# A macaron block with 32 experts: the down projection as three fp32r passes, one period later, with weights requested on GpSimd's word

## The reference

```python
x = x + 0.5 * ffn(_layernorm(x))
x = x + attention(_layernorm(x))
x = x + 0.5 * ffn(_layernorm(x))
...
# inside ffn, x normed once more (RMS), T = 4096 tokens, E = 32 experts, top 4 of them
probs = softmax(x @ w_router);  w_topk, sel = top_k(probs, 4)
# each expert takes its first CAP = 128 tokens, in order of token
buf = rows of x that expert e takes               # (32, 128, 256)
g = einsum('ech,ehf->ecf', buf, w_gate)           # f = 176
u = einsum('ech,ehf->ecf', buf, w_up)
y = einsum('ecf,efh->ech', silu(g) * u, w_down)   # (32, 128, 256)
out = zeros.at[tok].add(y[taken] * w_topk)
sh = silu(x @ sw_gate) * (x @ sw_up) @ sw_down    # shared expert, width 704
return inp + out + sigmoid(x @ w_shared_gate) * sh
```

## Time and profile before

| | before |
|---|---|
| device time, median of 3 runs | 938.1 us |
| the profiled execution, its own time | 938.85 us |
| its span | 937.0 us |
| TensorE busy | 909.6 us (97%) |
| VectorE busy | 695.9 us (74%) |
| ScalarE busy | 531.3 us (57%) |
| GpSimd busy | 511.1 us (55%) |
| TensorE's granted clock, mean | 0.999 |

### The profile page before, as it was taken

How to read it: one execution, slowest core, us unless ns; L and a number is a source line. 1 busy time by engine, 2 the same in 40 slices (tenths; PEclk the granted TensorE clock), 3 DMA queues, 4 the chain that set the end, 5 groups by cost and what they waited for, 6 DMA issues and landing times.

```text
span 937.0 us, 18000 instructions
## 1 busy us (share of the span) xinstructions
PE 909.6 (97%) x6118; PEld 685.6 (73%) x6118; DVE 695.9 (74%) x1704; ACT 531.3 (57%) x794; POOL 511.1 (55%) x537
## 2 busy tenths in 40 slices
PE   7999999999999999999999999989999999999997
PEld 6878887777778856666666666558788878777786
DVE  6998787555355889989998999988887875544435
ACT  6666743132233478878887888876667531322322
POOL 6343305565553588887888788934432055555530
PEclk9999999999999999999999999999999999999999
DMA  7143247777783610011001002004432377777735
GB/s 260 46 138 109 74 131 183 172 178 174 185 199 59 202 47 24 23 35 32 23 23 41 26 12 79 24 12 131 142 99 73 97 203 173 175 182 177 173 35 178
DMA packets 95512, 101.89 MB, mean 109 GB/s; under 512 B 18768, under 2 KB 86736, under 8 KB 95440
## 3 DMA queue, kind: packets, MB, share of 16 engines
q1 hardware_dynamic: 83152, 83.17, 29.5%
q0 software_dynamic: 12288, 17.83, 11.2%
HBM read 65.44 MB, written 35.54 MB: 108 GB/s over the span
## 4 chain that ended last, share of the span: by engine, by line
PE 63%; DVE 18%; issue 9%; ACT 4%; POOL 4%; DMA 1%; DVEq 0%; POOLq 0%; ACTq 0%
PE zT L1050 7%; PE gu L90 6%; PE gu L92 6%; PE gu L91 6%; PE gu L1070 6%; PE pj_at L90 3%; PE pv_at L1765 3%; PE pj_at L92 3%; PE pj_at L91 3%; PE down L90 3%; PE down L92 3%; PE down L91 3%; PE scores_at L1749 2%; PE zT L1059 2%; DVE turned_at L2007 2%
## 5 line engine op out<-in xcount | busy, mean ns | idle before, releaser
L90 PE MATMUL gu<-x_hi,gu_hi 128*128 128x512 f32 x264 | 120.4, 456 | 0.8 <-DVE act_gu L1353 0.7
L825 POOL DMA_INDIRECT rows<-z_rows,slots x64 | 69.3, 1083 | 67.9 <-DVE slots L1344 48.9
L1867 ACT ACTIVATE capped_at<-scores_at 128x2048 f32<-128x2048 f32 x64 | 93.1, 1454 | 20.5 <-PE scores_at L1749 20.3
L1130 ACT CAST a_hi<-act_gu 128x512 fp32r<-128x512 f32 x96 | 59.2, 617 | 79.1 <-DVE act_gu L1353 65.9
L92 PE MATMUL gu<-x_lo,gu_hi 128*128 128x512 f32 x264 | 103.9, 393 | 0.0
L91 PE MATMUL gu<-x_hi,gu_lo 128*128 128x512 f32 x264 | 103.6, 393 | 0.0
L1875 ACT ACTIVATE probs_at<-capped_at 128x2048 f32<-128x2048 f32 x64 | 95.1, 1487 | 2.5
L90 PE MATMUL down<-down_hi,a_hi 128*128 128x256 f32 x300 | 93.9, 313 | 0.6 <-DVE a_lo L1363 0.4
L1944 POOL TENSOR_SCALAR_AFFINE_SELECT probs_at<-probs_at 128x1024 f32<-128x1024 f32 x64 | 85.5, 1340 | 9.7 <-ACT probs_at L1875 9.0
L1050 PE MATMUL zT<-w_gu,xT 128*128 128x352 f32 x256 | 86.3, 460 | 0.0
L1232 ACT ACTIVATE y<-gu,rows 128x256 f32<-128x256 f32 x64 | 30.3, 473 | 98.5 <-PE gu L1070 89.0
(11 more groups left out here) (262 smaller groups left out, 2603.3 us busy)
## 6 DMA issues: line engine op xcount, KB each, us to landing
w_gu<-in_w_gate SPq DMA_DIRECT2D x64, 176.0 KB, 2.7
w_gu<-in_w_up SPq DMA_DIRECT2D x64, 176.0 KB, 3.3
w_down<-in_w_down SPq DMA_DIRECT2D x64, 176.0 KB
z_rows<-z SPq DMA_DIRECT2D x16, 512.0 KB, 3.6
acc<-base SPq DMA_DIRECT2D x10, 512.0 KB, 3.4
out<-base SPq DMA_DIRECT2D x10, 512.0 KB, 3.3
xn_at<-acc SPq DMA_DIRECT2D x16, 256.0 KB, 2.8
x<-xn_at SPq DMA_DIRECT2D x16, 256.0 KB, 2.1
```

The lines of the kernel that those rows point to most:

```text
L90: nc.tensor.matmul(out, w_hi, x_hi, start=first, stop=False)
L825: pool.indirect_dma_start(out=gathered_rows[:, n, :], out_offset=None, in_=m.z_rows, in_offset=bass.IndirectOffsetOnAxis(ap=slots[:, e:e + ...
L1867: nc.scalar.activation(capped[:, u % 2, :, 0:n], scores[:, :, 0:n], ACT.Tanh, scale=QK_SCALE / SOFTCAP).then_inc(capped_ready, 1)
```

## The change

The diff, cut to the parts that run in the second half of the feed-forward stage. Lines are the same in both feed-forward stages.

```diff
-        prodT = sb("prodT", [FD, 2, 2, CAP], F32)
-        y = sb("y", [P, HELD_Y, C], F32)
-        w_down = sb("w_down", [FD, HELD_W, 2, C], F32)
+        xT = sb("xT", [P, 2, KC, CAP], F32)
+        prodT_hi = sb("prodT_hi", [FD, 2, CAP], F32R)
+        prodT_lo = sb("prodT_lo", [FD, 2, CAP], F32R)
+        w_down = sb("w_down", [FD, HELD_D, 2, C], F32)
+        w_down_hi = sb("w_down_hi", [FD, 2, 2, C], F32R)
+        w_down_lo = sb("w_down_lo", [FD, 2, 2, C], F32R)
...
             def load_down(e):
-                sp.dma_start(w_down[:, e % HELD_W, :, :], ins["w_down"][e].rearrange("(p k) n -> p k n", k=2)
-                             ).then_inc(w_down_loaded[e % HELD_W], 16)
+                at_least(sp, w_down_lo_made, e - HELD_D + 1)
+                sp.dma_start(w_down[:, e % HELD_D, :, :], ins["w_down"][e].rearrange("(p k) n -> p k n", k=2)
+                             ).then_inc(w_down_loaded[e % HELD_D], 16)
...
             for e in range(HELD_W, E):
+                reached(sp, weights_due, e - HELD_W + 1)
+                load_down(e - 1)
                 reached(sp, gu_done, e - HELD_W + 1)
                 load_gate_up(e)
-                reached(sp, y_ready, e - HELD_W + 1)
-                load_down(e)
+            load_down(E - 1)
...
             for e in range(E):
                 add(e)
+                if e + HELD_W < E:
+                    pool.memset(tick[:, e:e + 1], 0.0).then_inc(weights_due, 1)
                 if e + HELD_ROWS < E:
...
-                at_least(pe, prodT_copied, e - 1)
+                at_least(pe, prodT_lo_ready, e - 1)
...
             def down_expert(e):
-                n = e % HELD_W
-                reached(pe, w_down_loaded[n], 16 * (e // HELD_W + 1))
-                reached(pe, prodT_copied, e + 1)
+                n = e % 2
+                reached(pe, w_down_lo_made, e + 1)
+                reached(pe, prodT_lo_ready, e + 1)
                 if e == 0:
                     reached(pe, lists_ready, 2)
                 at_least(pe, y_scaled, e)
                 for k in range(2):
-                    last = nc.tensor.matmul(y_ps, prodT[:, e % 2, k, :], w_down[:, n, k, :], start=k == 0, stop=k == 1)
+                    last = split_matmul(nc, y_ps, prodT_hi[:, k, :], prodT_lo[:, k, :], w_down_hi[:, n, k, :],
+                                        w_down_lo[:, n, k, :], k == 0, k == 1)
                 last.then_inc(y_ready, 1)
...
                 slot(b, *ROUTES[b])
             lead()
             for e in range(E):
+                if e == 1:
+                    down_expert(0)
+                gate_up_expert(e)
                 if e + 1 < E:
                     turn_rows(e + 1)
-                gate_up_expert(e)
-                *earlier_pieces, last_piece = pieces_beside(e)
-                for p in earlier_pieces:
+                first_piece, *later_pieces = pieces_beside(e)
+                piece(first_piece)
+                if e > 1:
+                    down_expert(e - 1)
+                turn_products(e)
+                for p in later_pieces:
                     piece(p)
-                turn_products(e)
-                piece(last_piece)
                 if e < 12 and e % 2 == 0:
                     find(2 + e // 2)
-                down_expert(e)
             for p in range(behind_experts, LAST_PIECE):
                 piece(p)
+                if p == behind_experts:
...
+            def high_products(e):
+                reached(act, prodT_ready, e + 1)
+                at_least(act, y_ready, e)
+                nc.scalar.copy(prodT_hi[:], prodT_ps).then_inc(prodT_hi_ready, 1)
+
+            def high_down(e):
+                reached(act, w_down_loaded[e % HELD_D], 16 * (e // HELD_D + 1))
+                at_least(act, y_ready, e - 1)
+                nc.scalar.copy(w_down_hi[:, e % 2], w_down[:, e % HELD_D]).then_inc(w_down_hi_made, 1)
...
+                if e == 1:
+                    scale(0)
                 silu_expert(e)
-                for p in pieces_beside(e):
+                first_piece, *later_pieces = pieces_beside(e)
+                followup(first_piece)
+                if e > 1:
+                    scale(e - 1)
+                high_products(e)
+                high_down(e)
+                for p in later_pieces:
                     followup(p)
-                scale(e)
             for p in range(behind_experts, LAST_PIECE + 1):
                 followup(p)
+                if p == behind_experts:
+                    scale(E - 1)
...
-            def copy_products(e):
-                reached(dve, prodT_ready, e + 1)
-                at_least(dve, y_ready, e - 1)
-                dve.tensor_copy(prodT[:, e % 2], prodT_ps).then_inc(prodT_copied, 1)
+            def low_products(e):
+                reached(dve, prodT_hi_ready, e + 1)
+                dve.tensor_tensor(prodT_lo[:], prodT_ps, prodT_hi[:].bitcast(F32), ALU.subtract).then_inc(prodT_lo_ready, 1)
+
+            def low_down(e):
+                reached(dve, w_down_hi_made, e + 1)
+                dve.tensor_tensor(w_down_lo[:, e % 2], w_down[:, e % HELD_D], w_down_hi[:, e % 2].bitcast(F32), ALU.subtract
+                                  ).then_inc(w_down_lo_made, 1)
...
             for e in range(E):
+                lists = e < 12 and e % 2 == 1
+                product_expert(e)
                 if e + 1 < E:
                     copy_rows(e + 1)
-                first, *middle, last_piece = pieces_beside(e)
-                followup(first)
-                product_expert(e)
-                for p in middle:
+                if lists:
+                    list_places(2 + e // 2)
+                first_piece, *later_pieces = pieces_beside(e)
+                followup(first_piece)
+                low_products(e)
+                if lists:
+                    list_tokens(2 + e // 2)
+                low_down(e)
+                for p in later_pieces:
                     followup(p)
-                copy_products(e)
-                followup(last_piece)
-                if e < 12 and e % 2 == 0:
-                    list_experts(2 + e // 2)
             for p in range(behind_experts, LAST_PIECE + 2):
                 followup(p)
```

More of the change, by code:

```diff
@@ L50 @@
 HELD_W = 4
+HELD_D = 3
 HELD_ROWS = 6
@@ L569, in ffn @@
         w_gu_loaded = [sem(f"w_gu_loaded{n}", 32 * (E // HELD_W)) for n in range(HELD_W)]
-        w_down_loaded = [sem(f"w_down_loaded{n}", 16 * (E // HELD_W)) for n in range(HELD_W)]
+        w_down_loaded = [sem(f"w_down_loaded{n}", 16 * len(range(n, E, HELD_D))) for n in range(HELD_D)]
+        w_down_hi_made = sem("w_down_hi_made", E)
+        w_down_lo_made = sem("w_down_lo_made", E)
         gathered = [sem(f"gathered{n}", 16 * len(range(n, E, HELD_ROWS))) for n in range(HELD_ROWS)]
@@ L577, in ffn @@
         prodT_ready = sem("prodT_ready", E)
[L578 removed]
+        prodT_hi_ready = sem("prodT_hi_ready", E)
+        prodT_lo_ready = sem("prodT_lo_ready", E)
         y_ready = sem("y_ready", E)
```

30 lines of the change are left out of this document (20 added, 10 removed).

## The result

| | us | profiled execution | its span | granted clock |
|---|---|---|---|---|
| before | 938.07 (937.97 to 940.89) | 938.85 | 937.0 | 0.999 |
| after | 946.94 (944.35 to 948.68) | 944.35 | 942.5 | 0.998 |

The ratio, taken over all executions, is 1.0085, with an interval of 1.0054 to 1.0116; by the medians the kernel is **slower by 8.9 us**, where 938 was forecast. The profiled execution is the fastest of the four; the others have spans of 944.6 to 946.8 at a mean granted clock of 0.995 to 0.996.

A forecast was written before the change was run, and what follows sets the result against it. TensorE, busy 97% of the span, was taken as the bound. Per stage 12.7 us won against 13.2 lost, twice 0.5, less 1.3 at the first stage's end, gave -0.3 on 938.85: 938 us, range 917 to 953.

The forecast's parts named there:

- A: Main forecast, experts of both stages: the new loop gives back what the passes save; own range 930 to 945, chance 0.50.
- slower: Summed chance that the whole kernel gets slower by more than the 0.3%, 2.8 us, indistinguishable from no change: 0.32.
- The passes and the order: Experts, per stage: six shorter down projection passes save 7.4 us, the vanished wait for the product 5.3, together 12.7.
- The loop: Experts, per stage: fixed order of new ScalarE and VectorE work makes TensorE wait, 13.2 us of waits in all.
- other waits for `xT`: Experts, per stage: TensorE waits for the row copy where a later piece ends a product, 4.5 us.
- lists: Experts, odd periods 9 and 11: lists cost TensorE waits of 1.1 us a stage.
- restarts: Experts, per stage: each restart after a wait costs TensorE about 0.06 us, twenty times, 1.2 in all.
- The end of the first stage: Last add lands about 4 us earlier, so the 1.3 us TensorE lacks behind 303 are covered: -1.3.
- B: Rival, experts: the loop is shorter or covered and the gain shows; 925 with half the waits, 912 with none; chance 0.23.
- C: Rival, experts: TensorE is tied to the adds and gets slower, 8.1 us a stage, 954 us; chance 0.19.
- D: Rival: TensorE gains nothing but the add's chain does, first stage ending 3 us earlier still, 935 us; chance 0.08.
- The memset: GpSimd's memset behind each add, taken at 0.2 us, hidden in its wait for the landing: costed at nothing.

The follow-up runs named there:

- After_early: The changed kernel with only attention's weights requested early (Wq, Wk, Wv ahead of the adds, Wo's parts one a period, experts 5 to 20): 945.23 us.
- the four edits of the loop: Changed kernel with rows copied before the product (940.36 us), down weights split early (939.11), both (935.35), or the split left out after two experts (939.59).
- weights_early: The changed kernel with ScalarE rounding the down weights right behind the expert's silu and VectorE subtracting them ahead of the product's low part: 939.11 us.
- word_alone: The kernel before with only its weights requested on GpSimd's word behind the add of four experts back: 939.00 us.
- both_y_down_first: Changed kernel, rows copied first, weights split early, attention's weights early, no GpSimd word, down loads awaiting an earlier down projection, down projection before the first piece: 923.59 us.
- order_alone: The changed kernel's order with two plain matmuls, the product copied as it is, no weight split and requests as before the change: 932.02 us.
- order_early: order_alone with attention's weights requested early (Wq, Wk, Wv ahead of the first add, Wo's parts at experts 5 to 20): 928.62 us.
- order_rows_early: order_early with VectorE copying the turned rows ahead of the expert's product: 928.00 us.
- split_alone: The kernel before with the three passes and the weights split behind silu and product, without the change of order, requests as before: 958.82 us.
- both_early: The changed kernel with rows copied first, down weights split early and attention's weights requested early: 932.40 us.

## Why the prediction was wrong

The forecast was 938 and the kernel took 946.94: inside the range of 917 to 953, but outside A's own 930 to 945, and slower, which had 0.32. The mechanism of forecast A held: the passes save, the loop takes it back. That it took back more, and by so much, comes from three sizes.

*The passes and the order: right.* Six passes start 0.12 apart, and periods in the down pieces without a wait take 3.64 to 3.75 and 4.43, against 3.76 and 4.47 forecast. The wait for the product went and the one for `xT` came.

*The loop: mis-sized by 2.0 us a stage, 4 in all.* Before's 141.43 less the 12.7 saved and the 0.71 moved out would be 128.0; the second stage took 143.26, so 15.2 us were lost where the forecast summed 13.2. The forecast's waits are counted from start to start, so TensorE's idle rows of that stage are compared with 0.16 added to each:

| us, second stage | measured | forecast |
|---|---|---|
| first two periods, for `xT` | 1.2 | 1.0 |
| other waits for `xT`, eight places (1.65 at expert 30) | 6.3 | 7.4 (4.5; lists 1.1; expert 30 1.8, taken for one for `a_lo`) |
| first low weights | 1.4 | 1.4 |
| low parts of a piece (0.78, 0.79; the rows name `a_hi` L1414) | 1.6 | 2.2 |
| `w_gu` 0.88, a piece's product 0.42 | 1.3 | nothing |
| the rest of 15.2, by subtraction | 3.4 | 1.2 (restarts) |

So the long links were sized well, some too high. What failed is "each restart after a wait costs TensorE about 0.06, twenty times: 1.2", and two waits that had no term. The 3.4 are mostly delays of 0.1 to 0.3 that no idle row of TensorE shows, such as transposes of the product that follow the down projection after 0.22 to 0.39 instead of 0.12; their causes were not tested one by one.

*The end of the first stage: the wrong sign, 1.8 us.* "The last add lands about 4 us earlier" took the adds' own step for what sets it. Before, the last add started 5.9 us behind the end of its scale (299.59 and 293.65), so the adds did set it. After the change they follow their scales by 0.75 to 2.4 us up to expert 28, so there TensorE's pace sets them. The last scale ends at 296.70, 3.1 later than before, since the experts are slower and the last down projection stands behind a piece; and the burst of attention's weights, which I had seen as a step of 6.17 and not priced, puts the adds 5 us behind their scales once more. Forecast -1.3, measured +0.5. After_early shows the burst's part: without it the add of expert 29 starts 1.4 behind its scale. Nor had I seen that the first stage passes on only a part: of the 3.4 to 6.2 us that its experts won in the four edits of the loop, 1.5 to 2.8 reached the second stage.

*The spread of the executions: no term at all, 2.6 us.* The median is 2.6 us over the profiled execution; three of before's four lie within 0.13. If all work went by the clock, a mean clock lower by 0.003 would be 2.8 us of 943. After_early shows a fall of the clock among the experts' first waits that cost 1.2; that the other three executions of the changed kernel had such falls is argued, not shown. The clock is not all of the spread either: two executions of weights_early had the same mean of 0.998 and spans of 934.4 and 942.0. What makes these executions differ stays open.

-0.3 forecast, + 4.0 + 1.8 gives the 5.5 of the profile, and 2.6 for the spread: 8.1, and 0.8 for before's profiled execution standing above its median gives 8.9.

*The rivals.* B came true only with both orders changed and then for a fifth of its price: 935.35 is 2.7 us under the forecast of 938, where B had 13. C was wrong here (gate and up waited for `w_gu` once, 0.7 us) and right for the mechanism: at a period below the adds' steps the word cost 5.7 us. The transfers' turns on shared engines, which the Trainium skill gives (DMA: Bandwidth & Descriptors, SWDGE vs HWDGE vs iDMA), agree with what the traces have without any word: in the kernel before, the step beside the burst of attention's weights was 6.17 us and those beside nothing 3.9 to 4.1; after the change they were 8.28 and 4.1 to 4.3. One step of before among the experts' own loads, from 223.26, was 6.17 as well. D held for the adds in word_alone: the last one came 2.8 us earlier and TensorE's stop behind 303 shrank from 1.30 to 0.27, but the whole time gained nothing. The memset, taken at 0.2 with bounds of 0.1 and 0.5, takes 0.55; with it the whole time changed by 0.9 us at most.

## What to carry to other kernels

Work moved to engines that are half idle is free only by its place in their order: walk the ring from one period's result to the next period's need, and put first what can start first (here the copy of rows and the split of weights), before asking what the new instructions cost. A gain counts only up to the next thing that all stages meet at: look there first (here the last add and the loads beside it), for it decides whether a period's gain reaches the end. And try the parts alone: here the order was the gain and the passes, placed badly, the loss.

## What the runs showed of the hardware

- An idle stretch of TensorE can be paid twice. In both_y_down_first it had no work from 300 to 303 and a granted clock of 0.50 from 303 to 306 and 0.67 to 310, that is mostly the lower of the two levels (1.2 GHz of 2.4); order_alone, idle from 301.3 to 306.9, had 0.50 from 306 to 310. Before and after the change, idle for 1.30 and 1.51 us at the same place, kept 1.00. In between it can go either way: order_early, idle for 2.64 us, had 0.71 from 303 to 306 and 0.79 to 310, and order_rows_early, idle for 2.59, kept 1.00.
- Some kernels spread and others don't: the changed kernel's runs lie 4.3 us apart, word_alone's ten within 0.33, split_alone's four within 0.14, both_early's four within 0.64; of before's, between 6 of 13 and 6 of 7 in a set lie within 0.3 us of the lowest, the others up to 5.3 above it. No run shows why.
- The same loads, requested at another moment against the indirect adds, changed the adds' mean step (4.8 to 4.9 against 4.6 to 4.7) and the whole time by 1.1% (942.41 and 931.92).
- A memset of a single word on GpSimd takes 0.55 us.
